# f32 operands for the mask products of the experts' first layer

## What is computed

```python
x = x + gat(layernorm(x))          # 8 heads, softmax over the edges of a node, relu
x = x + ffn0(layernorm(x))         # 32 experts, each node by one
x = x + relations(layernorm(x))    # 16 relations: transformed[rel, src] * weight, summed by dst
x = x + ffn1(layernorm(x))         # 8 experts, two for all nodes, gelu, layernorm
```

```python
idx = argmax(xf @ router_w.T + router_b)
h = relu(xf @ W1[idx] + b1[idx])    # 256 -> 64, 32 experts
out = relu(h @ W2[idx] + b2[idx])   # 64 -> 256
```

## Time and profile before

| | |
|---|---|
| median of 3 runs | 3556.42 us (3555.38 to 3558.89) |
| the profiled execution | 3553.55 us, span 3551.9 us |
| mean granted clock of TensorE in it | 0.793 of full speed |
| TensorE busy | 2038.9 us (57%) |
| VectorE | 1808.5 us (51%) |
| ScalarE | 757.0 us (21%) |
| GpSimd | 1954.4 us (55%) |
| pipeline of `attention` on TensorE | about 413 to 2008 us of the span |

### The profile page before, as it was taken

How to read it: one execution, slowest core, us unless ns; L and a number is a source line. 1 busy time by engine, 2 the same in 40 slices (tenths; PEclk the granted TensorE clock), 3 DMA queues, 4 the chain that set the end, 5 groups by cost and what they waited for, 6 DMA issues and landing times. The chain is left out here.

```text
span 3551.9 us, 37123 instructions
## 1 busy us (share of the span) xinstructions
PE 2038.9 (57%) x7510; PEld 1302.1 (37%) x7510; DVE 1808.5 (51%) x4035; ACT 757.0 (21%) x1428; POOL 1954.4 (55%) x1920
## 2 busy tenths in 40 slices
PE   1600399999999999999979500000000000369996
PEld 1400266565666656666546200000000000346664
DVE  7643765555556666566530254544454444314545
ACT  3200133333333333333223200000000000013331
POOL 5434874455655767777710277777777777300111
PEclk9955699999999999999989855555555555579998
DMA  6536344445555555554522533333333333100000
GB/s 237 212 102 179 86 126 136 142 135 155 144 146 152 146 166 149 168 165 143 150 87 76 173 106 106 105 106 105 106 105 105 105 105 105 45 30 12 18 18 25
DMA packets 209182, 416.09 MB, mean 117 GB/s; under 512 B 53562, under 2 KB 96018, under 8 KB 208930
## 3 DMA queue, kind: packets, MB, share of 16 engines
q0 software_dynamic: 87168, 239.28, 25.3%
q1 hardware_dynamic: 114706, 167.99, 13.3%
q10 hardware_dynamic: 7056, 6.63, 0.5%
HBM read 259.06 MB, written 154.68 MB: 116 GB/s over the span
## 5 line engine op out<-in xcount | busy, mean ns | idle before, releaser
L822 POOL DMA_INDIRECT gat_rows<-h_table,gat_idx x824 | 923.2, 1120 | 468.8 <-issue 246.0
L1412 POOL DMA_INDIRECT rel_rows<-transformed,rel_idx x824 | 779.1, 945 | 258.2 <-issue 258.2
L1042 PE MATMUL bank<-tr_wr,tr_xt 128*128 128x512 f32 x1568 | 725.1, 602 | 33.8 <-ACT tr_row L913 28.9
L1584 PE MATMUL bank<-weight,rec 128*128 128x1 f32 x196 | 42.0, 352 | 1073.0 <-DVE weight L1610 1073.0
L1584 PEld LDWEIGHTS bank<-weight,rec 128*128 128x128 f32 x196 | 41.9, 333 | 1073.8 <-DVE weight L1610 1073.8
L1009 PE MATMUL bank<-mo_xt,mo_w 128*128 128x256 f32 (+1 forms) x1600 | 429.1, 392 | 1.6 <-ACT mo_ones L894 1.6
L1487 DVE SCALAR_TENSOR_TENSOR bank<-rel_rows,rel_now,bank 128x256 f32<-128x256 f32 x823 | 403.1, 490 | 51.6 <-DVE bank L1487 27.0
L1042 PEld LDWEIGHTS bank<-tr_wr,tr_xt 128*128 128x128 f32 x1568 | 294.4, 192 | 322.9 <-issue 276.4
L913 ACT ACTIVATE tr_row<-bank 128x512 f32<-128x512 f32 x392 | 233.7, 597 | 678.1 <-PE bank L1042 665.5
L1027 PE MATMUL bank<-mo_w,mo_ht 128*128 128x256 f32 x1568 | 366.7, 380 | 0.0
L1009 PEld LDWEIGHTS bank<-mo_xt,mo_w 128*128 128x128 f32 x1600 | 286.3, 192 | 133.0 <-issue 101.2
(11 more groups left out here) (274 smaller groups left out, 2034.7 us busy)
## 6 DMA issues: line engine op xcount, KB each, us to landing
transformed<-tr_row SPq DMA_DIRECT2D x392, 256.0 KB, 2.4
windows<-win SPq DMA_DIRECT2D x34, 736.0 KB, 3.2
gat_rows<-h_table,gat_idx POOLq DMA_INDIRECT x824
rel_rows<-transformed,rel_idx POOLq DMA_INDIRECT x824, 2.8
h_table<-hrow ACTq DMA_DIRECT2D x49, 132.0 KB, 2.1
xa<-x SPq DMA_DIRECT2D x1, 6272.0 KB, 23.9
rec<-x_moved SPq DMA_DIRECT2D x1, 6272.0 KB
tr_x<-records SPq DMA_DIRECT2D x24, 256.0 KB, 4.1
```

The source lines that it names most:

```text
L822: pool.indirect_dma_start(out=rows[:, column(u, j), :], out_offset=None, in_=p.h_table[:], in_offset=bass.IndirectOffsetOnAxis(ap=idx[u][: ...
L1042: ins = pe.matmul(p.bank[6 + c % 2][:], xt2[:, k, u * P:(u + 1) * P], wr[:, k, m * CW:(m + 1) * CW], start=(k == 0), stop=(k == KD - 1))
L1412: pool.indirect_dma_start(out=rows[b][:, j, :], out_offset=None, in_=p.transformed[:], in_offset=bass.IndirectOffsetOnAxis(ap=idx[b][:, j: ...
```

## The change

The tiles `other` and `nots` are allocated as f32 instead of bf16. Everything that writes and reads them stays as it is: the instructions of lines 893, 1113 and 1003 have f32 outputs or operands instead of bf16 ones.

```diff
-        other = sb("mo_other", [E0, E0, H0], BF16)
+        other = sb("mo_other", [E0, E0, H0], F32)
...
-        nots = sb("mo_nots", [E0, PT], BF16)
+        nots = sb("mo_nots", [E0, PT], F32)
```

## The result

The changed kernel takes 3691.22 us (3688.44 to 3694.66, 5 runs) against 3556.42 us (3554.27 to 3558.89, 5 runs): a ratio of 1.0381, 95% interval 1.0367 to 1.0396, or **+134.8 us**. Forecast were 3678 us and +122. The profiled execution took 3694.66 us with a span of 3693.0 us; it is the slowest of the five, and that of before lay 2.9 us under its median, so the two traces differ by 141.1 us, some 6 more than the medians.

What follows compares the result with a forecast made beforehand. TensorE was taken to bound the mask phase until the gathers lead near its end, then again after them. Pairs 0 to 17 give 106 us, the tail 15, the table 1: +122 on 3556.42, 3678 us, range 3656 to 3704.

Steps and rivals of the forecast that it cites:

- The term of the mask products: TensorE's f32 masks, priced by the f32 bias product: +0.74 us per bank, eight banks making +5.9 us per pair.
- (b): Rival: the loss at the masks comes from mixing types and goes; +0.33 us a bank, 3613 us, chance 0.08.
- (c): Rival: losses belong to the type change and 32-row f32 is cheap; -0.31 us a bank, 3519 us, chance 0.02.
- The edits beside it: VectorE's table write as f32 counted at +1 us (0 to 1.1), ScalarE's one-hot write at nothing.
- The gather side: GpSimd's gathers stay 13.9 us behind pair starts while TensorE leads, then lead; their chain moves as a block, +106 us.
- the expected 5 to 15: Sign: TensorE's longest wait for an evacuation falls from 21.9 to between 5 and 15 us.
- the gathers as free from tile 42 on: From tile 42, 13.9 us after pair 18 starts, gathers go at their own pace; the tile starts 106 us later.
- the 69.2 us a pair: The gathers' own pace from tile 42: 138.4 us for four tiles, 69.2 per pair against 68.9 on TensorE.
- what I called hidden: The 5.9 us of each of pairs 18 to 21, 24 us together, fall into 31 us of existing TensorE waits.
- rival (a): Nothing is hidden: late gathers stay tied to TensorE, every pair passes on 5.9 us; 146 us, 3702 us, chance 0.08.
- both first pairs pass on 5.9 us each: In pairs 0 and 1 TensorE is last too, so each adds the full 5.9 us.
- a source of spread: Start of the phase, where TensorE still pauses between pairs: some us, within a forecast spread of 3656 to 3698 us.

Runs made afterwards that it cites:

- e1: Kernel before with bf16 mask operands filled with zeros from 32 to 128 rows: 4397.47 us against 4435.82 for the kernel before, ratio 0.9918.
- e2: Changed kernel with f32 mask operands filled with zeros to 128 rows: 4528.41 us against 4435.82 for the kernel before, ratio 1.0208.
- e4: Kernel before with both mask types written, f32 masks used in pairs 0 and 1 only: 4406.17 us against 4385.51 for the kernel before, ratio 1.0049.
- e8: The changed kernel itself, run on another chip: 4566.43 us against 4432.15 for the kernel before there, ratio 1.0309.
- e5: Kernel before with both mask types written, f32 masks in pairs 18 to 21 only: 4457.16 us against 4432.15 for the kernel before, ratio 1.0063.
- the control: Kernel before with both mask types written but bf16 masks used in all pairs: 4394.33 us against 4385.51 for the kernel before, ratio 1.0023.

## Why the prediction was right

It was right in direction, size and range, and the chain of steps held in the body; 13 us were missing, and the steps at both ends of the phase were too small.

The term of the mask products, +0.74 us a bank and 5.9 us a pair, came out as +0.73 and 5.89. It rested on a row of the same shape and type elsewhere in the phase, and not on the row of a first-layer product, by which it would have been +0.33. e1 and e2 show why this row was the right one: what it holds beyond its columns belongs to the change between 128 and 32 rows. Rivals (b) and (c), which put the loss on mixed types, fall with that. By the rule cited there from the Trainium skill ("TensorE: Matmul & The Clock Gate", "Why this matters for your kernels"), K=32 as dear as K=128, the kernel would have been at 3613 us; the records of e2 and of the change agree with it within a run (0.215 us each), but going from 128 rows to 32 and back costs 0.30 us a bank with bf16 masks and 0.39 with f32 ones (e1, e2), which the rule does not have.

The edits beside it: ScalarE's write takes 359 ns as before, and VectorE's table 1.22 us as before, so the 1 us that I put on it was not spent there. The table's write already begins 1.6 us later than before (316.53 against 314.91), so nearly all of the 1.7 us ahead of pair 0 comes from ahead of the edit.

```profile
316.53 1.22 DVE L1113 TENSOR_SCALAR mo_other<-ident 32x2048 f32<-32x2048 f32 x1
```

The gather side: the distance between TensorE and the gathers stayed at about 13.9 us while TensorE led (13.3), and then grew less than before (19.8 for 23.0 at pair 20). TensorE's longest wait fell to 15.6 us, at the edge of the expected 5 to 15. From pair 18 to the release +4.4 us were added where I had 0. I had taken the gathers as free from tile 42 on. They were held up once more, for 10.2 us where it was 1.8, and the four tiles took 144.2 us instead of 138.4 (1643.51 to 1787.73); without these waits they took 134.1 against 136.6, so the 69.2 us a pair that I took for their own pace is not a fixed one. So a part of what I called hidden was passed on, 4.4 of 23.6 us, and rival (a) was true to that part. No other run tests it: on the other chips the gathers do not lead in these pairs (they wait 177 to 207 us for sums there, whatever the kernel).

The step that was mis-sized is the start, "both first pairs pass on 5.9 us each". They passed on 22.2 us in the traces and not 11.8, beside the 1.7 us that lie ahead of them. At the 1.2 GHz level a mask group costs twice as much more as I took, +1.46 us instead of +0.74, as the first one shows, 2.00 us (417.77 to 419.77) against 0.54 (416.08 to 416.62) in the trace of before:

```profile
417.77 2.07 PE L1003 MATMUL bank<-mo_nots,mo_other 32*128 32x256 f32 x4
419.77 3.78 PE L1009 MATMUL bank<-mo_xt,mo_w 128*128 128x256 f32 x8
```

and TensorE stayed at that level for longer, which slowed everything else of these pairs too. From the mean clocks of the 24 us behind the two starts (0.85 and 0.89, then 0.70 and 0.58) I estimate 24 x 0.46 = 11.0 us of time at full speed lost, as much as the 10.4 us that are missing. I had named this stretch as a source of spread and put no number on it.

What kept TensorE at the low level for longer stays open. The f32 masks alone do not do it: with them it is back at 2.4 GHz nearly as early as with bf16 ones in e4 and e8. It may be chance of the profiled execution, but then only in part, since the other four are only 2 to 6 us below it (3688.44 to 3692.57 against 3694.66).

## What to carry to other kernels

Price a product by a row of the same type and the same number of rows among like neighbours: the columns and passes are one part, and the change from 128 rows to 32 and back another 0.3 to 0.4 us (products of 256 columns), and filling a 32-row operand up to 128 rows with zeros takes that away at no cost in time (2.25 to 1.95 us a bank). An f32 product where bf16 is exact (here 0, -1 and 2^100) buys nothing: it doubled both the records and the time of each. And before a new cost is booked as hidden in an engine's wait, look at who waits for what that engine does ahead of the wait: of 23.6 us booked so, 4.4 came through on the first chip, and about 17 in e5, where the gathers had free time too. A phase that begins behind a pause of TensorE is to be priced at the granted clock of that stretch (0.85 and 0.89 here, and as low as 0.58), not at full speed.

## What the runs showed that I had not expected

The same kernel took 3556 us on one chip and 4385 to 4436 us on the others, with no difference in the code; whether it is the chip or something else about those executions, no run shows. Of the 872 us between the two traces of the changed kernel (3693.0 and 4565.3), 520 lie between the starts of its first and its last pair, 38 ahead of them and 314 behind. In that phase pairs 2 to 21 of the control take 74 to 106 us, with pauses of TensorE that the profile ascribes to "issue" or to ScalarE, and pair 22 takes 62.9 us, once the gathers are over. What these pauses are, the profile does not tell. The change cost 135 us on the first chip and 134 (119 to 155) on another, though only on the first TensorE was busy all the time.
